# A graph layer's edge loop: fewer loads issued by SyncE, half of the table loads by ScalarE, and the pieces of the MLP values subtracted by TensorE instead of GpSimd

## The chip, the cores and the metric

The kernel runs on one core of a Trainium2 chip. Its time is the device time in microseconds of one execution; a lower one is better. PE is TensorE, DVE VectorE, ACT ScalarE, POOL GpSimd and SP SyncE, which computes nothing and issues DMAs.

## What is computed

412,500 edges join 12,500 nodes with 32 features each. For each edge two small MLPs turn ten edge features into weights, which then mix the features of its two nodes; the results are summed into the receiving node, and the layer ends in a layer norm.

```python
def _mlp(emb, w1, w2):
    h = jax.nn.relu(emb @ w1 / jnp.sqrt(jnp.float32(w1.shape[0])))
    return h @ w2 / jnp.sqrt(jnp.float32(w2.shape[0]))
...
xs, xd = (x[edge_src], x[edge_dst])
w = _mlp(emb, fc1_w1, fc1_w2)          # 512 values per edge, from 16 hidden ones
...
s_t = a1 * (jnp.einsum('eu,euw->ew', s1, Wss) + jnp.einsum('eu,euw->ew', vdot1, Wvv))
v_t = a1 * (jnp.einsum('eu,euw->ew', s1, Wsv)[:, :, None] * sh1[:, None, :] + jnp.einsum('euk,euw->ewk', v1, Wvs))
w2 = _mlp(emb, fc2_w1, fc2_w2)         # 384 values per edge
...
edge_out = jnp.concatenate([jnp.tanh(scal), (vecs * jnp.tanh(gates)[:, :, None]).reshape(E, 24)], axis=1)
edge_out = edge_out * norm[:, None]
return jax.ops.segment_sum(edge_out, edge_dst, num_segments=num_nodes)
```

## The kernel before

**Super tiles and stages.** The edges are sorted by receiver and cut into 403 super tiles of 8 x 128. `periods` runs one body for each: bodies of the first and last tiles written out, and a loop of two bodies (even and odd, for the double buffers) in between. A body works at six stages at once, on six super tiles: `three_on` and `four_on` are three and four ahead (embeddings are loaded and cut), `zero` two ahead (nodes gathered, hidden layer computed), `one` one ahead, `two` in its first products, `three` in its second ones, `four` at its outputs. Each engine has its own program of bodies, in an order written out by hand, and waits on semaphores.

**Pieces.** A float32 value is cut into three bf16 pieces, each the rounded rest of the one before. The pieces of the embeddings are stacked in six groups of ten rows in `emb_stack` (`stack_emb`, line 527, from `emb_parts`), those of the hidden values in six groups of 16 columns in `hid_parts`. ACT rounds (`emb_first`, `emb_second`, `hidden_first`, `hidden_second`), POOL subtracts (`emb_less_first`, `emb_less_second`, `hid_less_first`, `hid_less_second`, lines 829 to 850). ACT's `hidden_out` first brings the hidden values out of the PSUM bank `pa`, which the matmuls of `hidden`, `hidden_near` and `nodes_made` share. SP then turns `hid_parts` with two transposing DMAs, one for each MLP (`turn_hid`, line 546), and PE's `fill` multiplies the result with the second weights.

**Tables.** A receiver's share of the first products comes from a table `t_rows` of one row for each node and hidden value, of which a tile needs a window of eight nodes. `load_near` (line 575) reads the first node of each of the eight tiles from `near_base` into a register and issues a load of that window. PE uses the windows in `receivers`. Every second body also adds 64 nodes to the table (`nodes_made`, `store_nodes`).

**Small loads.** Each body loads the sender indices for the gathers (`load_indices`), the bases (`load_near_bases`), the offsets of the receivers for the one-hot matrices (`load_late`) and the base of the window of sums (`load_late_base`). All of these, the loads of `emb`, the six of the stack and the off rows (`stack_off`) stand in SP's queue; POOL issues the eight gathers of node rows.

**The order around.** PE's body is: fill 1 of `two`, `scalar_sums_turned`, `out_sums` (16 matmuls), `receivers`, `hidden`, `four_sums_turned`, fill 2 of `three`, `vector_sums`, `hidden_near` first half, fill 3, `scalar_sums`, second half, fill 4, `vector_sums_turned`, `scatter`, `nodes_made`, fill 0 of `one`, `gate_sums` (16 matmuls). ACT's is: `scalar_sums_back`, `emb_first`, `out_sums_out` (writes `osum_t`), `node_scalars` (a copy of the receivers' result), `tanh_out`, `hidden_out`, the copies of the node rows, `emb_second`, `hidden_first`, `vector_sums_out`, `near_hidden`, `hidden_second`, `off_hots`, `near_hidden` of the second half, `scalar_sums_out`, `nodes_out`, `one_hot`, `gate_sums_out`.

## Time and profile before

| | |
|---|---|
| median of 3 runs | 9704.65 us (9703.06 to 9709.19) |
| profiled execution | 9652.08 us, its span 9650.3 us |
| PE, PEld, DVE, ACT, POOL busy | 64%, 59%, 49%, 35%, 48% of the span |
| chain of work that ended last | SP's queue 76%, issue 19% |
| granted TensorE clock, mean | 0.788 of full speed |

Issuing DMAs doesn't count as busy, so SP has no share in the table; its queue is seen in the order of time and in the chain. "Issue" is time in which a queue stood at nothing that the profile shows, between two instructions. The lines of the profile are those of the code above.

### The profile page before, as it was taken

The page shows a single profiled execution, that of the slowest core. Times are in us where ns is not written, and L with a number is a line of the kernel's source. Part 1 is how long each engine was busy: PE and PEld are TensorE (multiplying, and loading weights), DVE is VectorE, ACT ScalarE, POOL GpSimd, SP SyncE. Part 2 cuts the span into 40 slices and gives each one's busy share as a digit, 9 for nine tenths or more (in the row PEclk, how much of TensorE's full clock was granted, in tenths as well). Part 3 has the DMA queues.
Part 4 walks back from the last instruction along what each step waited for, and adds up shares of the span by engine and source line. Part 5 has one row for each costly group of instructions (what it writes and reads, how often), then busy time and mean ns, then how long its engine had stood idle before and what let it go on. Part 6 is the DMA issues. An engine that isn't in the chain of part 4 may idle for free.

```text
span 9650.3 us, 223031 instructions
## 1 busy us (share of the span) xinstructions
PE 6180.1 (64%) x59272; PEld 5695.5 (59%) x59272; DVE 4712.0 (49%) x7823; ACT 3364.6 (35%) x10591; POOL 4658.2 (48%) x6483
## 2 busy tenths in 40 slices
PE   2566666666666666666666666666666666666666
PEld 2465665656656566565655656566565665656555
DVE  6344444444444444444444444444444444444445
ACT  2333333333333333333333333333333333333333
POOL 1545454454544545445454454545445454454543
PEclk6777787777878778777787877778777787877877
DMA  4222222222222222222222222222222222222222
GB/s 124 51 54 53 54 55 54 54 53 55 54 54 54 54 55 53 54 54 54 55 53 54 54 54 55 53 54 54 54 55 53 55 53 54 55 54 54 53 54 49
DMA packets 1898444, 535.96 MB, mean 56 GB/s; under 512 B 1783541, under 2 KB 1880551, under 8 KB 1898045
## 3 DMA queue, kind: packets, MB, share of 16 engines
q1 hardware_dynamic: 1795228, 482.38, 22.8%
q0 software_dynamic: 103168, 53.03, 3.8%
q8 instruction: 19, 0.31, 0.0%
q14 instruction: 29, 0.24, 0.0%
HBM read 203.14 MB, written 72.13 MB: 29 GB/s over the span
## 4 chain that ended last, share of the span: by engine, by line
SPq 76%; issue 19%; PE 2%; DVE 1%; DMA 1%; POOL 1%; ACT 0%; POOLq 0%; DVEq 0%; ACTq 0%
SPq L536 19%; SPq L585 15%; SPq L586 14%; SPq L556 10%; SPq L526 4%; SPq L606 2%; SPq L564 2%; SPq L544 2%; SPq L596 2%; SPq L573 2%; SPq L592 1%; SPq L612 1%; PE p L1355 1%; SPq L446 1%; DVE prods L1626 1%
## 5 line engine op out<-in xcount | busy, mean ns | idle before, releaser
L855 POOL DMA_INDIRECT nodes<-x_rows,idx x3224 | 3094.8, 960 | 732.9 <-issue 673.5
L1350 PE MATMUL pw<-w_stack,work 128*128 128x128 bf16 x16120 | 1466.6, 244 | 3032.0 <-DMA work<-hid_parts 2998.4
L1355 PE MATMUL p<-identity,prods 128*128 128x128 f32 x20956 | 3177.5, 314 | 0.6 <-ACT gates_t L1060 0.5
L1350 PEld LDWEIGHTS pw<-w_stack,work 128*128 128x128 bf16 x16120 | 1174.0, 110 | 3390.5 <-issue 3095.3
L1355 PEld LDWEIGHTS p<-identity,prods 128*128 128x128 f32 x20956 | 2886.8, 168 | 1.8 <-issue 1.7
L1689 DVE TENSOR_TENSOR prods<-pw,V 128x1024 f32<-128x1024 f32 x403 | 493.6, 1225 | 2813.4 <-PE pw L1350 2813.4
L832 POOL TENSOR_TENSOR emb_rest<-emb,emb_parts 80x128 f32<-80x128 f32 x403 | 171.6, 426 | 3232.5 <-ACT emb_parts L971 3225.7
L1060 ACT ACTIVATE gates_t<-p 128x128 f32<-128x128 f32 x403 | 111.7, 277 | 4285.8 <-PE p L1355 4285.8
L1775 DVE TENSOR_TENSOR along<-p,r_all 128x192 f32<-128x192 f32 x403 | 144.2, 358 | 1726.2 <-ACT th L1070 1726.2
L1733 DVE TENSOR_TENSOR prods<-pw,M 128x1024 f32<-128x1024 f32 x806 | 976.9, 1212 | 1.6 <-PE pw L1350 1.6
L1337 PE MATMUL pz<-work 128*128 128x64 f32 x6448 | 767.9, 272 | 10.3 <-DMA work<-t_rows 10.0
L1337 PEld LDWEIGHTS pz<-work 128*128 128x128 f32 x6448 | 755.0, 193 | 10.7 <-issue 10.2
L1077 ACT ACTIVATE spare<-node_iota,late_off 128x42 f32<-128x42 f32 x3224 | 747.7, 314 | 0.0
L1741 DVE TENSOR_TENSOR prods<-pw,VT 128x1536 f32<-128x1536 f32 x403 | 705.0, 1749 | 0.5 <-PE pw L1350 0.5
L806 POOL TENSOR_TENSOR msg<-th,w_all 128x128 f32<-128x128 f32 x403 | 164.2, 408 | 755.4 <-ACT th L1070 755.4
L1020 ACT ACTIVATE work<-pa 128x512 f32<-128x512 f32 x806 | 468.2, 581 | 0.8 <-PE pa L1313 0.7
L1706 DVE TENSOR_TENSOR prods<-pw,S 128x512 f32<-128x512 f32 x403 | 278.8, 692 | 269.5 <-PE pw L1350 266.0
L1007 ACT ACTIVATE hid_parts<-hid 128x768 bf16<-128x768 f32 x403 | 336.4, 835 | 0.0
L1434 PE MATMUL p<-spare,msg 128*32 128x42 f32 x6448 | 322.0, 203 | 1.7 <-DVE msg L1785 1.7
L1065 ACT ACTIVATE osum_t<-p 128x256 f32<-128x256 f32 x403 | 154.4, 383 | 474.9 <-PE p L1355 455.0
L1313 PE MATMUL pa<-emb_stack,w_near 96*128 96x512 bf16 x806 | 308.0, 382 | 1.8 <-ACT work L1020 1.3
L1038 ACT ACTIVATE prods<-pz 128x64 f32<-128x64 f32 x403 | 114.4, 284 | 557.9 <-PE pz L1337 557.9
(174 smaller groups left out, 8232.2 us busy)
## 6 DMA issues: line engine op xcount, KB each, us to landing
work<-t_rows SPq DMA_DIRECT2D x3224, 32.0 KB
t_rows<-t_stage SPq DMA_DIRECT2D x205, 256.0 KB
nodes<-x_rows,idx POOLq DMA_INDIRECT x3224
emb_stack<-emb_parts SPq DMA_DIRECT2D x2418, 20.0 KB
emb<-in_emb_t SPq DMA_DIRECT2D x403, 40.0 KB
work<-hid_parts SPq DMA_TRANSPOSE x806, 2.9
idx<-rec SPq DMA_DIRECT2D x403, 4.0 KB, 1.7
near_base<-base_rows SPq DMA_DIRECT2D x403, 0.0 KB
```

Of the source, the lines that this page charges most:

```text
L536: sp.dma_start(emb_stack[K1 * g:K1 * g + K1, p, :].rearrange("k (c e) -> k c e", c=G), emb_parts[:, p, part, :]).then_inc(stack_in[p], 16)
L556: sp.dma_start_transpose(hid_t[:, layer, p, :, :], hid_parts[:, p, layer * G:layer * G + G, :].rearrange("e t k -> e (t k)")).then_inc(tur ...
L585: first = nc.sync.value_load(near_base[0:1, p, t:t + 1], min_val=0, max_val=N - 1)
L586: sp.dma_start(t_near[:, p, t, :], t_rows[bass.ds(first * H, NEAR * H), :]).then_inc(t_near_in[p], 16)
L855: nc.gpsimd.indirect_dma_start(nodes[:, p, t, :], None, x_rows, bass.IndirectOffsetOnAxis(ap=idx[:, p, t:t + 1], axis=0)).then_inc(nodes_i ...
L1077: nc.scalar.activation(off_hot[:, t, :], node_iota[:, :], ACT.Square, bias=off[:, t:t + 1]).then_inc(off_hot_done, 1)
L1337: mm = nc.tensor.matmul(z[:, :, t, :], hid_near[:, P * t:P * t + P], t_near[:, a.par, t, :].rearrange("p (c w) -> p c w", w=C), start=(t = ...
L1350: mm = nc.tensor.matmul(pw[:, slot, t, :], hid_t[:, layer, a.par, t, :], w2_stack[:, lo:lo + W], start=True, stop=True)
L1355: return nc.tensor.matmul(out, column, identity[:, :], start=first, stop=last, is_transpose=True)
L1689: nc.vector.tensor_tensor(prod_v01.rearrange("p u k t w -> p k t u w"), weights(0, ring, 0).unsqueeze(1).broadcast_to([P, 2, G, C, C]), V[ ...
L1733: nc.vector.tensor_tensor(prod_g[:, :, half, :, :].rearrange("p u t w -> p t u w"), weights(2 + half, ring), M[:, a.par, :, :].unsqueeze(3 ...
L1741: nc.vector.tensor_tensor(prod_o[:, :, 0:3, :, :].rearrange("p u k t w -> p k t u w"), weights(4, ring, 1).unsqueeze(1).broadcast_to([P, 3 ...
```

## The change

- **Stacks.** `store_emb` stores the three pieces of `emb_parts` with one DMA in a DRAM tensor `emb3`. In the next body `stack_emb` waits for it and loads the stack with three DMAs, of three, two and one pieces. The off rows are loaded one body later too.
- **Small loads.** One record of indices and offsets for four super tiles (`load_records`) and one row of bases for four (`load_bases`) replace four loads; each body loads them anew, and the users take the slot of their stage. `load_bases` waits for the readers of the buffer on ACT and DVE (`windows_begun`, `window_begun`).
- **Table loads.** `load_windows` reads four bases with one load of registers and issues four windows. SP does this for tiles 0 to 3, and ACT, in a `load_near` of its own behind `out_sums_out`, for tiles 4 to 7.
- **Pieces of the hidden values.** They stay in PSUM. ACT writes the first piece three times straight from there, with ReLU and a factor a little under one, so that the rest stays positive; PE adds the piece times minus identity to the bank (`hidden_less`); ACT writes the second piece twice, PE subtracts it, ACT writes the third. `hidden_out` and POOL's two subtractions are gone, and `hidden_near` waits for the third piece (`hid_c`) where it waited for `hid_done`. The factor for the ten inputs moves into the second weights.

SP, in the loop's first body, from the table loads to the stacks. Before, with the first of the eight table loads and the end of the last:

```order
L585 TENSOR_LOAD near_base [waits t_stored]
L585 ISA x2
L586 ISA
L586 DMA work<-t_rows 128x64
...
L586 DMA work<-t_rows 128x64
L573 ISA
L573 DMA near_base<-base_rows 1x8
L556 DMA_TRANSPOSE work<-hid_parts 128x8x128 [waits hid_c,hid_a,hid_b,filled_b]
L606 ISA [waits off_hot_done]
L606 DMA late_off<-rec 128x8
L536 DMA emb_stack<-emb_parts 10x8x128 [waits hid_mm,emb_c,near_mm]
L536 DMA emb_stack<-emb_parts 10x8x128 x5
```

After, from the same place, with the first of four table loads, up to the stacks in the next body:

```order
L522 TENSOR_LOAD near_base [waits t_stored]
L522 ISA x8
L525 ISA
L525 DMA work<-t_rows 128x64
...
L612 ISA [waits windows_begun]
L612 DMA near_base<-base_rows 1x32
L581 DMA_TRANSPOSE work<-hid_parts 128x8x128 [waits hid_c,hid_a,hid_b,filled_b]
L450 ISA [waits emb_c]
L547 DMA emb3<-emb_parts 80x3x128 [waits stack_in1]
L581 DMA_TRANSPOSE work<-hid_parts 128x8x128 [waits hid_c,hid_a,hid_b,filled_e]
L560 DMA emb_stack<-emb3 30x1024 [waits near_mm]
L560 DMA emb_stack<-emb3 20x1024
```

Four issues and seven register loads are gone, late offsets too; one store stands where six stack issues stood, and the three that fill the stack stand in the next body.

ACT, between the copy of the out sums (`osum_t`) and the first piece of the hidden values. Before:

```order
L1065 ACTIVATE osum_t<-p2 128x256 [waits four_back,osum_sum]
L1036 REGISTER_ALU
L1038 ACTIVATE prods<-pz 128x64 [waits sv_done,d_mm]
L1070 ACTIVATE th<-p1 128x128 [waits msg_done,four_back]
L991 REGISTER_ALU
L996 ACTIVATE hid<-pa 128x8x2x16 [waits hid_a,hid_rest_done,hid_mm]
```

After, where three more pairs like the last `ISA` and `DMA` stand ahead of the copy from `pz`:

```order
L1088 ACTIVATE osum_t<-p2 128x256 [waits four_back,osum_sum]
L450 REGISTER_ALU [waits near_base_in1,d_mm]
L522 TENSOR_LOAD near_base [waits t_stored]
L522 ISA x8
L525 ISA
L525 DMA work<-t_rows 128x64
L1061 ACTIVATE prods<-pz 128x64 [waits sv_done,d_mm]
L1093 ACTIVATE th<-p1 128x128 [waits msg_done,four_back]
L1029 ACTIVATE hid_parts<-pa 128x16x48 [waits turned_in10,turned_in00,hid_mm]
```

The table loads came in ahead of the dot copy and tanh, and the first piece (line 1029) follows tanh at once, out of `pa`.

PE, from the turning of the four sums to fill 3. Before:

```order
L1427 MATMUL p1<-identity,gates_t 128x128 [waits msg_done]
L1429 MATMUL p1<-identity,osum_t 128x128 x2
L1350 MATMUL pw<-w2_stack,work 128x128 [waits turned_in11,pss_done]
L1350 MATMUL pw<-w2_stack,work 128x128 x7
L1355 MATMUL p2<-identity,prods 128x128 [waits pv_done]
L1355 MATMUL p2<-identity,prods 128x128 x3
L1313 MATMUL pa<-emb_stack,w1_near 128x512 [waits t_out,hid_done]
L1350 MATMUL pw<-w2_stack,work 128x128 [waits turned_in11,pc_done,pvv_done]
```

After:

```order
L1472 MATMUL p1<-identity,gates_t 128x128 [waits msg_done]
L1474 MATMUL p1<-identity,osum_t 128x128 x2
L1346 MATMUL pa<-hid_parts,minus_bf 128x256 [waits hid_a]
L1395 MATMUL pw<-w2_stack,work 128x128 [waits turned_in11,pss_done]
L1395 MATMUL pw<-w2_stack,work 128x128 x7
L1400 MATMUL p2<-identity,prods 128x128 [waits pv_done]
L1400 MATMUL p2<-identity,prods 128x128 x3
L1346 MATMUL pa<-hid_parts,minus_bf 128x256 [waits hid_b]
L1358 MATMUL pa<-emb_stack,w1_near 128x512 [waits t_out,hid_c,off_in1]
L1395 MATMUL pw<-w2_stack,work 128x128 [waits turned_in11,pc_done,pvv_done]
```

A subtraction stands ahead of fill 2 and another behind the vector sums, each with a wait for ACT.

```diff
-    c1 = 1.0 / (4.0 * 32.0 ** 0.5)
-    c2 = 1.0 / (4.0 * 4.0)
+    c1 = float(K1) ** -0.5 / (4.0 * 32.0 ** 0.5)
+    c2 = float(K1) ** -0.5 / (4.0 * 4.0)
+    below = 1.0 - 2.0 ** -8
...
+    emb3 = nc.dram_tensor("emb3", [2, 3, K1, SUPER], BF16, kind="Internal").ap()
...
-        hid_rest = sb("hid_rest", [P, 2 * G, H])
+        minus_bf = sb("minus_bf", [P, P], BF16)
...
+        def load_windows(eng, p, t0):
+
+            half = G // 2
+            _, firsts = nc.values_load_multi_w_load_instructions(
+                near_base[0:1, p, 3 * G + t0:3 * G + t0 + half], engines=[eng.engine], min_val=0, max_val=N - 1)
+            for t in range(half):
+                eng.dma_start(t_near[:, p, t0 + t, :], t_rows[bass.ds(firsts[t] * H, NEAR * H), :]
+                              ).then_inc(t_near_in[p], 16)
...
-            def stack_emb(a, is_general=True):
+            def store_emb(a):
 
                 p = a.par
-                if not is_general:
+                sp.wait_ge(emb_c, a.n(1, 1))
+                sp.sem_inc(begun, 1)
+                wait(sp, stack_in[p], a.before(2).k(16 * 3))
+                sp.dma_start(emb3[p].rearrange("a k (c e) -> (k c) a e", c=G), emb_parts[:, p, :, :]).then_inc(emb_stored[p], 16)
+
+            def stack_emb(a, is_general):
+
+                p = a.par
+                sp.wait_ge(emb_stored[p], a.k(16))
+                sp.sem_inc(begun, 1)
+                if is_general:
+                    wait(sp, hid_mm, a.before(2).n(1, 1))
+                else:
                     wait(sp, near_mm, a.before(2).n(2, 2))
-                sp.wait_ge(emb_c, a.n(1, 1))
-                wait(sp, hid_mm, a.before(2).n(1, 1))
-                for g, part in enumerate((0, 1, 2, 0, 1, 0)):
-                    sp.dma_start(emb_stack[K1 * g:K1 * g + K1, p, :].rearrange("k (c e) -> k c e", c=G),
-                                 emb_parts[:, p, part, :]).then_inc(stack_in[p], 16)
+                first = 0
+                for parts in (3, 2, 1):
+                    sp.dma_start(emb_stack[K1 * first:K1 * (first + parts), p, :],
+                                 emb3[p, 0:parts].rearrange("a k e -> (a k) e")).then_inc(stack_in[p], 16)
+                    first += parts
...
+            def load_records(at, i, is_general):
+
...
+                if i is None or 0 <= i + 1 < NS:
+                    sp.wait_ge(nodes_in[1 - p], At(at.b, at.d + 1).k(16 * G))
+                    sp.sem_inc(begun, 1)
+                if not is_general:
+                    wait(sp, off_hot_done, at.before(2).n(G, G))
+                    sp.sem_inc(begun, 1)
+                sp.dma_start(near[:, p, lo:hi, :], rec[:, bass.ds(at.index() + lo, hi - lo), :]).then_inc(near_in[p], 16)
+
...
+            def load_bases(at, i):
+
...
+                wait(sp, window_begun, at.n(1, -2))
+                sp.sem_inc(begun, 1)
+                wait(sp, windows_begun, at.n(1, 1) if i is None else min(i + 1, NS))
+                sp.sem_inc(begun, 1)
+                sp.dma_start(near_base[:, p, G * lo:G * hi],
+                             base_rows[:, bass.ds((at.index() + (lo - 1)) * G, (hi - lo) * G)]).then_inc(near_base_in[p], 16)
...
-                for t in range(G):
-                    first = nc.sync.value_load(near_base[0:1, p, t:t + 1], min_val=0, max_val=N - 1)
-                    sp.dma_start(t_near[:, p, t, :], t_rows[bass.ds(first * H, NEAR * H), :]).then_inc(t_near_in[p], 16)
+                load_windows(nc.sync, p, 0)
...
                     if four_on is not None:
                         load_emb(four_on)
-                    if three_on is not None:
-                        load_indices(three_on, is_general)
-                    if three is not None and not is_general:
-                        load_late_base(three)
+                    load_records(at, i, is_general)
+                    if three_on is not None and is_general:
+                        load_destinations(three_on)
                     if one is not None and not is_general:
                         load_near(one)
-                    if three_on is not None and not is_general:
-                        load_near_bases(three_on)
+                    if not is_general:
+                        load_bases(at, i)
                     if one is not None and i != -1:
                         turn_hid(one, 0)
-                    if two is not None:
-                        load_late(two, is_general)
+                    if two is not None and is_general:
+                        load_late_destinations(two)
                     if three_on is not None:
-                        stack_emb(three_on, is_general)
-                        if not is_general:
-                            stack_off(three_on)
+                        store_emb(three_on)
...
-            def hid_less_first(a):
...
-            def hid_less_second(a):
-                pool.wait_ge(hid_b, a.n(1, 1))
-                nc.gpsimd.tensor_tensor(hid_parts[:, a.par, :, KH - H:KH], hid_rest[:, :, :],
-                                        hid_parts[:, a.par, :, 3 * H:4 * H], ALU.subtract).then_inc(hid_c, 1)
...
-            def hidden_out(a, is_general):
+            def parts_of(a):
+                return hid_parts[:, a.par, :, 0:KH].rearrange("p a (g h) -> p a g h", h=H)
+
+            def hid_of(copies):
+                return hid_ps.unsqueeze(2).broadcast_to([P, 2 * G, copies, H])
+
+            def hidden_first(a, is_general):
+
                 act.wait_ge(hid_mm, a.n(1, 1))
-                wait(act, hid_rest_done, a.before(2).n(1, 1))
-                wait(act, hid_a, a.before(2).n(1, 1))
-                if is_general:
-                    wait(act, t_prods_done, a.before(2).n(G, G))
-                nc.scalar.activation(hid[:, a.par, :, :].rearrange("p (l t) h -> p t l h", l=2),
-                                     hid_ps.rearrange("p t (l h) -> p t l h", l=2), ACT.Relu,
-                                     scale=float(K1) ** -0.5).then_inc(hid_done, 1)
-
-            def hidden_first(a):
-                act.wait_ge(hid_done, a.n(1, 1))
                 for layer in range(2):
                     wait(act, turned_in[layer][a.par], a.before(2).k(16))
                 if a.static and a.b * 2 + a.d == 0:
                     act.wait_ge(parts_zero, 3)
-                parts = hid_parts[:, a.par, :, 0:KH].rearrange("p a (g h) -> p a g h", h=H)
-                nc.scalar.activation(parts[:, :, 0:3, :], hid[:, a.par, :, :].unsqueeze(2).broadcast_to([P, 2 * G, 3, H]),
-                                     ACT.Copy).then_inc(hid_a, 1)
+                if is_general:
+                    wait(act, t_prods_done, a.before(2).n(G, G))
+                    nc.scalar.activation(hid[:, a.par, :, :], hid_ps, ACT.Relu).then_inc(hid_done, 1)
+                nc.scalar.activation(parts_of(a)[:, :, 0:3, :], hid_of(3), ACT.Relu, scale=below).then_inc(hid_a, 1)
 
             def hidden_second(a):
-                parts = hid_parts[:, a.par, :, 0:KH].rearrange("p a (g h) -> p a g h", h=H)
-                act.wait_ge(hid_rest_done, a.n(1, 1))
-                nc.scalar.activation(parts[:, :, 3:5, :], hid_rest[:, :, :].unsqueeze(2).broadcast_to([P, 2 * G, 2, H]),
-                                     ACT.Copy).then_inc(hid_b, 1)
+                act.wait_ge(hid_less, a.n(2, 1))
+                nc.scalar.activation(parts_of(a)[:, :, 3:5, :], hid_of(2), ACT.Relu, scale=below).then_inc(hid_b, 1)
+
+            def hidden_third(a):
+                act.wait_ge(hid_less, a.n(2, 2))
+                nc.scalar.activation(parts_of(a)[:, :, 5, :], hid_ps, ACT.Relu).then_inc(hid_c, 1)
...
+            def load_near(a):
+
+                p = a.par
+                act.wait_ge(near_base_in[p], a.k(16))
+                act.sem_inc(begun, 1)
+                wait(act, d_mm, a.before(2).n(1, 1))
+                act.sem_inc(begun, 1)
+                wait(act, t_stored, a.before(1).k(16, 16 * (LEAD - 1)))
+                act.sem_inc(begun, 1)
+                load_windows(nc.scalar, p, G // 2)
+                act.sem_inc(windows_begun, 1)
...
+                    if one is not None and fast:
+                        load_near(one)
                     if two is not None:
                         node_scalars(two)
                     if four is not None:
                         tanh_out(four)
                     if zero is not None:
-                        hidden_out(zero, is_general)
+                        hidden_first(zero, is_general)
                     if one is not None:
                         row_scalars(one)
                         row_vectors(one)
                     if three_on is not None:
                         emb_second(three_on)
                     if zero is not None:
-                        hidden_first(zero)
+                        hidden_second(zero)
                     if two is not None:
                         vector_sums_out(two)
+                    if zero is not None:
+                        hidden_third(zero)
                     if one is not None and fast:
                         near_hidden(one, 0)
-                    if zero is not None:
-                        hidden_second(zero)
                     if marking is not None:
...
+            def hidden_less(a, piece, made):
+
+                pe.wait_ge(made, a.n(1, 1))
+                slot = (0, 3)[piece]
+                nc.tensor.matmul(hid_ps, minus_bf[:, :], hid_parts[:, a.par, :, slot * H:slot * H + H], start=False,
+                                 stop=True, skip_group_check=True).then_inc(hid_less, 1)
...
                         hidden(zero, is_general)
                     if four is not None:
                         four_sums_turned(four, windows, more)
+                    if zero is not None:
+                        hidden_less(zero, 0, hid_a)
                     if three is not None:
                         if two is not None:
                             pe.wait_ge(pss_done, two.n(1, 1))
...
                         fill(three, 2, at.par)
                     if two is not None:
                         vector_sums(two, four)
+                    if zero is not None:
+                        hidden_less(zero, 1, hid_b)
                     if one is not None and fast:
                         hidden_near(one, 0)
...
-                        dve.wait_ge(late_base_in[four.par], four.k(16))
+                        dve.wait_ge(near_base_in[1 - four.par], four.k(16, 32 if four.par else 16))
                         dve.sem_inc(begun, 1)
-                        first = nc.vector.value_load(late_base[0:1, four.par, 0:1], min_val=0, max_val=N - 1)
+                        first = nc.vector.value_load(near_base[0:1, 1 - four.par, 0:1], min_val=0, max_val=N - 1)
+                        dve.sem_inc(window_begun, 1)
```

## Rows read from the trace of the kernel before

**Rows 1.** The page: busy time of the engines (parts 1, 3 and 4)

```profile
PE 6180.1 (64%) x59272; PEld 5695.5 (59%) x59272; DVE 4712.0 (49%) x7823; ACT 3364.6 (35%) x10591; POOL 4658.2 (48%) x6483
...
q1 hardware_dynamic: 1795228, 482.38, 22.8%
...
SPq 76%; issue 19%; PE 2%; DVE 1%; DMA 1%; POOL 1%; ACT 0%; POOLq 0%; DVEq 0%; ACTq 0%
```

**Rows 2.** Who waited for whom: engine, line, releaser, us, times, longest

```profile
PE pw L1350 <- DMA work<-hid_parts: 2998.4, 401, 9.5
```

**Rows 3.** SP in order of time: start us, us, line, operation

```profile
5007.03 0.59 SPq L592 DMA_DIRECT2D t_rows<-t_stage  x1
5009.27 0.90 SPq L526 DMA_DIRECT2D emb<-in_emb_t  x1
5010.48 0.36 SPq L564 DMA_DIRECT2D idx<-rec  x1
...
5012.87 8.29 SPq L586 DMA_DIRECT2D work<-t_rows  x8
...
5024.18 4.94 SPq L536 DMA_DIRECT2D emb_stack<-emb_parts  x6
...
5055.61 0.90 SPq L526 DMA_DIRECT2D emb<-in_emb_t  x1
```

**Rows 4.** Lines 585 and 586, table loads: duration ns min/median/max

```profile
L585 SPq TENSOR_LOAD <-near_base x16: 263/268/465, 5011.9 to 5041.9; - x16
...
L586 SPq DMA_DIRECT2D work<-t_rows x2904: 337/338/368, 1002.6 to 9399.3; - x194
```

**Rows 5.** PE in order of time: two bodies at full clock, one at half

```profile
3360.16 0.61 PE L1350 MATMUL pw<-w_stack,work 128*128 128x128 bf16 x8
3360.61 0.39 PE L1396 MATMUL pz<-halves,st_t 128*128 128x64 f32 x2
3360.83 1.92 PE L1355 MATMUL p<-identity,prods 128*128 128x128 f32 x16
...
3364.71 0.33 PE L1427 MATMUL p<-identity,gates_t 128*128 128x128 f32 x1
...
3365.09 0.61 PE L1350 MATMUL pw<-w_stack,work 128*128 128x128 bf16 x8
...
3366.85 0.38 PE L1313 MATMUL pa<-emb_stack,w_near 96*128 96x512 bf16 x1
...
3371.12 0.38 PE L1254 MATMUL pa<-wt,xt 48*64 48x256 bf16 x2 [0.48 <-ACT work L1020]
...
3379.63 3.62 PE L1355 MATMUL p<-identity,prods 128*128 128x128 f32 x16
```

**Rows 6.** ACT in order of time, the same body

```profile
3362.79 0.38 ACT L1065 ACTIVATE osum_t<-p 128x256 f32<-128x256 f32 x1 [1.20 <-PE p L1355]
...
3365.29 0.28 ACT L1070 ACTIVATE th<-p 128x128 f32<-128x128 f32 x1 [0.49 <-PE p L1429]
...
3366.42 0.84 ACT L1007 ACTIVATE hid_parts<-hid 128x768 bf16<-128x768 f32 x1
...
3367.42 0.60 ACT L1020 ACTIVATE work<-pa 128x512 f32<-128x512 f32 x1
...
3368.64 1.86 ACT L1077 ACTIVATE spare<-node_iota,late_off 128x42 f32<-128x42 f32 x8
```

**Rows 7.** GpSimd by line, 500 to 9500 us: busy us, mean ns, idle before

```profile
L844 POOL TENSOR_TENSOR hid_rest<-hid,hid_parts 128x256 f32<-128x256 f32 x388 | 264.5, 682 | 8.1
```

**Rows 8.** The page, DMA issues: KB each, median us to landing

```profile
work<-hid_parts SPq DMA_TRANSPOSE x806, 2.9
idx<-rec SPq DMA_DIRECT2D x403, 4.0 KB, 1.7
```

**Rows 9.** PE in order of time, before the loop

```profile
204.31 0.60 PE L1254 MATMUL p<-wt,xt 48*64 48x256 bf16 x2 [4.43 <-ACT t_stage L1025]
...
217.57 0.38 PE L1254 MATMUL p<-wt,xt 48*64 48x256 bf16 x2 [3.09 <-ACT t_stage L1025]
```

119 lines of the change are left out of this document (57 added, 62 removed).

## The prediction

> **What bounds the kernel now.** I read the engine shares first, then the chain of work that ended last, then who waited for whom, and last the order in time of two bodies of the loop. No compute engine is busy for more than 64% of the span, and the chain stands on SP's queue for 76% of it [rows 1]. PE's largest wait, 2998 us, is for the transposing DMA that SP issues [rows 2]. The order in time shows why: SP goes from issue to issue without a pause, and two bodies take 5055.61 - 5009.27 = 46.34 us [rows 3]. That is 23.17 us for each of the 403 super tiles, so 9,338 us of the span; the rest, about 310 us, is the part before and after, which the change hardly touches. SP's queue is therefore a serial program of issue times. An issue taken off it is worth its full time until another loop is longer.
>
> **What leaves SP.** One body of SP as it is [rows 3]: six stack issues in 4.94 us (0.82 each), eight table issues in 8.29 us (1.14 from one to the next), of which the register load is 0.27 [rows 4].
> - Four table loads go to ACT: 4 x 1.14 = 4.6. The four that stay share one register load, so three are saved: 3 x 0.27 = 0.8.
> - Six stack issues become three: -2.5. In their place one store to DRAM. No row shows it. The nearest are the 64-partition store at 0.59 (5007.03) and the 80-partition load at 0.90 (5009.27); with its wait I take 1.1, and 0.6 to 2 as ends.
> - The small loads of the late base and of the late offsets go. Each is like the index load, 0.36 long (5010.48); with what surrounds them I take 0.7 and 0.6.
> - More waits on semaphores: +0.3.
> SP's own work becomes 23.2 - 4.6 - 0.8 - 2.5 + 1.1 - 0.7 - 0.6 + 0.3 = 15.4 us a body. If nothing else set the pace, that would be 403 x 7.8 = 3,140 us less.
>
> **The next loop: PE, ACT and DVE.** I take a body where PE ran at the full clock and set 0 at its turning of the four sums, 3364.71 [rows 5]. From that point to the matmul of nodes_made (3371.12) are 6.4 us, to the fill behind it some 6.7. From such a fill to the next zero: the fill itself 0.45 (as from 3360.16 to 3360.61), sixteen gate sums 1.8 (as the out sums, 1.92 long and overlapping), and 3364.71 - 3360.16 = 4.55 for fill, out sums, receivers and hidden. That is 6.8, so a round without stall would be 13.5 us. Today the gate sums after the stall run at half clock (3.62 in place of 1.92), which then ends.
>
> *ACT's four table loads.* They stand behind osum_t, which ends at 3363.17, that is -1.5 [rows 6], and in front of the dot copy, tanh and the first pieces. On SP such a block costs one load, four pairs of register checks and four issues: 4 x 1.14 - 3 x 0.27 = 3.8 us. No row shows ACT issuing a DMA, and its queue also has activations to pass on, so I take a little over SP: 4.1. Ends: 1.3, where it would fit in the time for which ACT waits for the receivers' matmuls anyway, and 6.0, if each issue cost a stack issue's 0.82. With 4.1 ACT is free at 2.6, tanh begins at 2.85 rather than 0.6 (3365.29), and the first pieces, 0.84 long, are out at 3.9 [rows 6].
>
> *PE's two subtractions.* Each is one matmul of 256 columns, about 0.2 us, half of the 0.38 of the 512-column one [rows 5]. The price is the waits in PE's order. The first stands before the fill of kind 2, which today starts 0.38 after the zero; now it waits for ACT's first pieces (3.9) and the fill starts at 4.2: +3.8, of which some 2.5 are ACT's loads. The second stands behind the vector sums, at 6.0, and ACT's second pieces are out at about 5.0. But hidden_near must now wait until ACT has read the bank a third time, since the values stay in PSUM: 6.2 + 0.4 = 6.6, so it starts at 6.7 where it started at 2.1. Behind it ACT copies it (0.6), makes the off hots (1.86), copies the second half (0.6) [rows 6]: with PE's 0.38 and the hand-overs 3.6 us to nodes_made, at 10.3, and the next fill at 10.5. The round is 10.5 + 6.8 = **17.3 us**. DVE (4712 / 403 = 11.7 us busy a body) is carried along, and ACT comes to 8.3 + 4.1 = 12.4 [rows 1].
>
> *GpSimd.* Two operations of 0.68 us leave each body [rows 7]. I cost their removal at nothing: POOL is busy 11.6 us a body today [rows 1], and with the pauses between its gathers its round is some 13 us. If ACT's work were free, POOL would still not be first.
>
> *Does SP come back?* SP waits every second body for ACT's node copy (0.85 after that fill), then issues store and xt (2.2), three stacks (2.7), off rows (0.6), emb (1.2), records (0.7), the first table load with its waits (1.35), the rest (2.9), bases (0.85, as the index load with its waits): 12.5; the transpose lands 2.9 later [rows 8]. That is 0.85 + 12.5 + 2.9 = 16.3, against 17.3 for which PE does not need it. So it is hidden, with 1.0 us to spare in two bodies.
>
> **The sum.** 403 x (23.17 - 17.3) = 2,370 us. The profiled execution took 9652.08, so its like would be 7,282. The median of the runs is 52.6 above that execution; 9704.65 - 2370 = **7,335 us**.
>
> **A rule weighed.** The packets of SP's queue take 22.8% of the 16 DMA engines' time [rows 1]. The Trainium skill, DMA: Bandwidth & Descriptors, section "Issuing engines are not separate DMA queues", says that a second issuing engine saves only the time to initiate a DMA, usually small beside the DMA itself. It would let one expect almost nothing from the move. Here the first half agrees with the trace and the second does not: the issue time is the bound.
>
> **Rivals.**
> 1. *ACT's loads are cheap, or much of them is hidden.* With 1.3 us for the block the PE round is 14.5, and SP's loop decides: (14.5 + 16.3) / 2 = 15.4 a body, 403 x 7.8, so 6,570 us. Between that and 17.3 lies 6,900 for a block of 3.0. For it: ACT waits there today. Against it: SP's issue rows are steady at 0.338.
> 2. *Issues collide.* Four issues on ACT fall into the stretch where SP issues its own; each waiting for one of 0.34 to 0.8 us adds about 1.9: 19.2 a body, 9704.65 - 403 x 3.97 = 8,105. The rows can't show it, as only SP issues such DMAs. The Trainium skill, Perfetto Trace Analysis, section "DMA Instruction - HWDGE (DVE, Sync)", says that the descriptor generator is shared and locked for one sequencer at a time; no trace here shows a lock wait.
> 3. *The clock falls in the new gap.* PE would idle from 0.55 to 4.0, some 3.4 us a body. After an idle stretch of 3.09 us the trace has a pair of matmuls in 0.38 us, at full clock; after 4.43 us it has 0.60 for the same pair [rows 9]. If the clock falls to its lower level in each body, fill and sums after the gap lose what they lose today, 1.7 + 0.4: 19.4 a body, 8,185 us.
> 4. *SP is in the way again.* If store, stack loads and landings cost 4 us a pair more than I took, the two bodies take 17.3 + 20.3: 18.8 each, 7,945 us.
> 5. *Slower than before.* The embedding pieces now go to DRAM and back. SP waits in its queue for the store to land before it issues the stacks, and everything behind stands. A body is then 13 us plus the landing time. It passes 23.17 when landing takes over 10.2 us; at 12 it gives 25.0 a body, 10,440 us. The nearest landing is 1.7 us for a small load [rows 8], so this is far away.
> 6. *No change.* If SP's issues were long because the transfers behind them were full, fewer issues would not help: 9,705 us. Constant issue times and idle DMA engines speak against it.
>
> **Chances.** The forecast, with block costs from 3.2 to 5.0 us (16.4 to 18.2 a body, 6,980 to 7,700 us), 0.50. Rival 1 0.17, rival 2 0.10, rival 3 0.11, rival 4 0.07, rival 5 0.03, rival 6 0.02. The range must take in rivals 2 and 3 and most of the way to rival 1, since no row shows an ACT issue: 6,750 to 8,190 us. Left out are about half of rival 1, rivals 5 and 6 and the far end of 3 and 4, less than 0.2. Within 0.2% is what a measurement of this kernel can tell from no change; faster than that 0.95, within it 0.02, slower 0.03.
>
> **What the profile after would show.** SP has pauses, with waits for ACT's node copy, and no longer holds the chain; PE's wait for the transposes (2998 us) falls to a few hundred or less. In its place stand a PE wait of about 3.4 us a body ahead of the first subtraction, on ACT's first pieces, and a short one ahead of hidden_near. ACT's dot copy starts about 4 us after osum_t rather than 1.7. The gate sums take 1.9 us. POOL waits longer, not shorter. The mean granted clock is above 0.9. I would be wrong if ACT's four issues take under 2 us (then 6,600 to 6,900), if the matmuls behind the gap take twice as long, or if PE still waits for the transposes.

## The result, and the profile after

The changed kernel takes **9094.31 us** (median of 4 runs, 9075.28 to 9110.34) against 9706.92 us: ratio 0.9368, 95% interval 0.9347 to 0.9389. It is faster, but by 6% and not by the 24% that I forecast (7335 us), and outside my range (6,750 to 8,190). Its profiled execution took 9084.12 us. With the 313 us around the loop (9650.3 - 403 x 23.17) a body takes (9081.9 - 313) / 403 = 21.8 us; I had taken 17.3.

The page of the changed kernel: engine shares, granted clock in 40 slices, DMA queues (q10 is the new one, which ScalarE issues to) and the chain that ended last. The rows of before are [rows 1]:

```profile
PE 6666.9 (73%) x60078; PEld 6007.7 (66%) x60078; DVE 4733.8 (52%) x7823; ACT 3365.5 (37%) x10591; POOL 4138.0 (46%) x5678
...
PEclk8788878788888888888888878887888888888877
...
q1 hardware_dynamic: 1428533, 464.10, 22.6%
...
q10 hardware_dynamic: 232128, 52.93, 2.6%
...
PE 56%; issue 18%; ACTq 13%; ACT 8%; another core or an unknown queue 3%; DVE 1%; SPq 1%; POOL 0%; DMA 0%; DVEq 0%; POOLq 0%
```

SP's queue has left the chain (76% before, 1% now), and PE holds it with ACT. The bound has moved as forecast. The waits say where it is dear (engine, line, releaser: us in all, times, longest):

```profile
DVE prods L1782 <- remote: 1923.5, 299, 7.2
...
PE pa L1346 <- ACT hid_parts L1029: 998.6, 400, 3.8
PE pa L1358 <- issue: 948.1, 403, 5.1
ACT vs_t L1066 <- remote: 889.3, 211, 6.4
...
SPq L580 <- PE pw L1395: 1937.7, 322, 8.5
```

No row is left of PE's wait for the transposes [rows 2]. PE waits 2.5 us a body for ACT's first pieces (L1346), as foreseen. The rest I had not foreseen: 2.4 us ahead of `hidden_near` (L1358), and DVE and ACT waiting for "remote", which means that nothing in the records had just ended when they were let go.

One body in order of time shows such a release: PE, then ACT, then POOL.

```profile
5002.37 0.33 PE L1472 MATMUL p<-identity,gates_t 128*128 128x128 f32 x1
...
5005.34 0.28 PE L1346 MATMUL pa<-hid_parts,minus_bf 128*128 128x256 bf16 x1 [2.42 <-ACT hid_parts L1029]
...
5005.90 1.48 PE L1400 MATMUL p<-identity,prods 128*128 128x128 f32 x12
5007.22 0.27 PE L1346 MATMUL pa<-hid_parts,minus_bf 128*128 128x256 bf16 x1
5010.44 0.58 PE L1358 MATMUL pa<-emb_stack,w_near 96*128 96x512 bf16 x1 [2.95 <-issue]
...
5016.31 0.38 PE L1291 MATMUL pa<-wt,xt 48*64 48x256 bf16 x2 [0.73 <-ACT work L1043]
...
5009.69 0.38 ACT L1066 ACTIVATE vs_t<-p 128x256 f32<-128x256 f32 x1 [3.25 <-remote]
...
5005.40 0.98 POOL L880 DMA_INDIRECT nodes<-x_rows,near  x1 [0.23 <-issue]
5006.69 0.94 POOL L880 DMA_INDIRECT nodes<-x_rows,near  x1 [0.30 <-issue]
...
5008.25 0.96 POOL L880 DMA_INDIRECT nodes<-x_rows,near  x1 [0.16 <-issue]
```

The vector sums (L1400) and the subtraction behind them (L1346) are over at 5007.5 by PE's own rows, yet ACT, which waits for nothing else, copies the sums at 5009.69. The trace's semaphore events have the sums' signal at 5009.66, 2.28 us behind the recorded end, and the subtraction's at 5009.70, 0.03 behind it, though that matmul is 0.27 long. So the signals are held and then come in a bunch. ACT starts 0.02 us behind the signal, so it is really let go that late. I call a TensorE completion **late** when its signal comes over 0.7 us behind the recorded end. Between 500 and 8500 us the changed kernel has 2067 late ones; the kernel before has 7.

The count takes the first recorded event of the semaphore at or behind the end, within 12 us, and some events have no record: 7 of 100 in the changed kernel, 1.5 in the kernel before, up to 24 elsewhere, none in the kernels without gathers. Where two matmuls raise one semaphore, the first is then counted late by the record of the second. In 306 of 368 bodies of the changed kernel this is so for the first half of `hidden_near`, though ACT's copy, which waits for it, starts 0.04 us behind its end. If each record is given only to the last matmul that it can belong to, 1746 late ones are left in the changed kernel and none of the 7 in the kernel before. In e2, e4 and e5c below 1266, 1083 and 528 are left, elsewhere nearly all; no reading below hangs on the difference.

The Trainium skill, Perfetto Trace Analysis, section "Summary: the profiler window per engine type", says that a TensorE end in the profile is estimated. Here the kernel before agrees with the estimate to 0.01 us throughout, so an end that differs by 2 us is a finding.

### The profile page after: what moved, and what is told of

It reads as the page before. It is cut to its first block, busy times and chain, and to the rows that moved or that the text cites. A ratio compares the mean times of both kernels' runs of the same rounds, so it can differ in the third digit from the quotient of the medians.

```text
span 9081.9 us, 221656 instructions
## 1 busy us (share of the span) xinstructions
PE 6666.9 (73%) x60078; PEld 6007.7 (66%) x60078; DVE 4733.8 (52%) x7823; ACT 3365.5 (37%) x10591; POOL 4138.0 (46%) x5678
## 4 chain that ended last, share of the span: by engine, by line
PE 56%; issue 18%; ACTq 13%; ACT 8%; another core or an unknown queue 3%; DVE 1%; SPq 1%; POOL 0%; DMA 0%; DVEq 0%; POOLq 0%
PE p L1400 31%; PE pw L1395 12%; ACTq L525 7%; ACTq L522 4%; PE pa L1358 4%; ACT hid_parts L1029 3%; PE pa L1346 2%; PE p L1479 2%; ACT spare L1100 2%; PE pa L1291 2%; ACT work L1043 1%; PE pz L1441 1%; DVE prods L1675 1%; PE pz L1423 1%
## 5 line engine op out<-in xcount | busy, mean ns | idle before, releaser
L880 POOL DMA_INDIRECT nodes<-x_rows,near x3224 | 3087.9, 958 | 851.9 <-issue 804.5
L1400 PE MATMUL p<-identity,prods 128*128 128x128 f32 x20956 | 3216.2, 316 | 0.6 <-ACT gates_t L1083 0.5
L1400 PEld LDWEIGHTS p<-identity,prods 128*128 128x128 f32 x20956 | 2879.0, 167 | 1.2 <-DVE prods L1796 0.7
L1395 PE MATMUL pw<-w_stack,work 128*128 128x128 bf16 x16120 | 1557.8, 253 | 7.2 <-DVE prods L1762 3.1
L1395 PEld LDWEIGHTS pw<-w_stack,work 128*128 128x128 bf16 x16120 | 1280.5, 115 | 288.8 <-issue 157.7
L1358 PE MATMUL pa<-emb_stack,w_near 96*128 96x512 bf16 x806 | 411.2, 510 | 948.1 <-issue 948.1
L1346 PE MATMUL pa<-hid_parts,minus_bf 128*128 128x256 bf16 x806 | 286.4, 355 | 1013.9 <-ACT hid_parts L1029 998.6
L1346 PEld LDWEIGHTS pa<-hid_parts,minus_bf 128*128 128x128 bf16 x806 | 92.1, 114 | 1109.0 <-ACT hid_parts L1029 1092.6
L1358 PEld LDWEIGHTS pa<-emb_stack,w_near 96*128 96x128 bf16 x806 | 92.7, 115 | 1094.9 <-issue 1094.9
L1100 ACT ACTIVATE spare<-node_iota,near 128x42 f32<-128x42 f32 x3224 | 748.7, 318 | 0.0
L1066 ACT ACTIVATE vs_t<-p 128x256 f32<-128x256 f32 x403 | 154.8, 384 | 1538.3 <-remote 889.3
```

What stands on the lines that cost most here:

```text
L880: nc.gpsimd.indirect_dma_start(nodes[:, p, t, :], None, x_rows, bass.IndirectOffsetOnAxis(ap=near[:, 1 - p, 3, t:t + 1], axis=0)).then_inc ...
L1100: nc.scalar.activation(off_hot[:, t, :], node_iota[:, :], ACT.Square, bias=off[:, t:t + 1]).then_inc(off_hot_done, 1)
L1346: nc.tensor.matmul(hid_ps, minus_bf[:, :], hid_parts[:, a.par, :, slot * H:slot * H + H], start=False, stop=True, skip_group_check=True).t ...
L1358: nc.tensor.matmul(near_ps, w1_near[:, :, :].rearrange("k n h -> k (n h)"), emb_stack[:, p, 512 * half:512 * half + 512], start=True, stop ...
L1395: mm = nc.tensor.matmul(pw[:, slot, t, :], hid_t[:, layer, a.par, t, :], w2_stack[:, lo:lo + W], start=True, stop=True)
L1400: return nc.tensor.matmul(out, column, identity[:, :], start=first, stop=last, is_transpose=True)
```

## The experiments

All against the kernel before on the same chip. "Body" is (span - 313) / 403, "late" as above, "clock" the mean granted TensorE clock. e6c ran on a chip on which the kernel before takes 9651.8 us; where the others ran it would take 7652 x 9707 / 9652 = 7696 us, which I use in differences. e6c, e11 and e14 leave the gathers out, so their node rows are not those of the senders and their results are other values.

| kernel | us | ratio (95%) | body | late | clock |
|---|---|---|---|---|---|
| before | 9707 | 1 | 23.2 | 7 | 0.79 |
| the change | 9094 | 0.937 (0.935 to 0.939) | 21.8 | 2067 | 0.81 |
| e1 POOL subtracts | 7737 | 0.795 (0.791 to 0.799) | 18.5 | 1444 | 0.91 |
| e2 all table loads on SP | 9202 | 0.948 (0.947 to 0.950) | 22.0 | 1543 | 0.84 |
| e3 both, SP's part alone | 7815 | 0.805 (0.803 to 0.806) | 18.7 | 1238 | 0.87 |
| e4 before, PE subtracts | 10956 | 1.129 (1.127 to 1.131) | 26.4 | 1327 | 0.77 |
| e6c the change, no gathers | 7652 | 0.793 (0.792 to 0.794) | 18.2 | 0 | 0.86 |
| e5c the change, gathers apart | 7869 | 0.811 (0.809 to 0.812) | 18.7 | 609 | 0.88 |
| e7c e1, gathers apart (0.2 us) | 7444 | 0.765 (0.761 to 0.769) | 17.8 | 1620 | 0.93 |
| e9 e1, gathers apart (0.4 us) | 7346 | 0.756 (0.755 to 0.758) | 17.6 | 1385 | 0.92 |
| e10 e4, gathers apart | 9714 | 1.0005 (0.9996 to 1.0015) | 23.3 | 21 | 0.83 |
| e8 e1, real work between gathers | 7095 | 0.730 (0.728 to 0.732) | 16.8 | 1692 | 0.95 |
| e12 e8, all table loads on SP | 7512 | 0.775 (0.773 to 0.776) | 17.9 | 838 | 0.90 |
| e11 e8, no gathers | 6487 | 0.668 (0.667 to 0.670) | 15.3 | 0 | 0.98 |
| e13 e8 and gathers apart | 6813 | 0.703 (0.700 to 0.705) | 16.0 | 489 | 0.96 |
| e14 e6c, ACT's loads later | 7963 | 0.821 (0.819 to 0.823) | 19.0 | 0 | 0.87 |

### Which part loses the time (e1 to e4)

e1 puts the two subtractions back on POOL, with `hidden_out`; e2 moves all eight table loads to SP; e3 does both; e4 is the kernel before with TensorE's subtraction.

```diff
 # e1 (POOL's body; ACT and PE as before the change)
                         gathers(zero, (2,))
+                        hid_less_first(zero)
                         gathers(zero, (3,))
...
                         gathers(zero, (4,))
+                        hid_less_second(zero)
                         gathers(zero, (5,))
 # e2
                 load_windows(nc.sync, p, 0)
+                load_windows(nc.sync, p, G // 2)
...
-                    if one is not None and fast:
-                        load_near(one)
```

> The changed kernel with one part undone: GpSimd subtracts the pieces of the MLP values again (ScalarE copies them from SBUF as before), SyncE and ScalarE load as in the change. In the changed kernel a body takes 21.8 us instead of the 17.3 us I had taken, and TensorE's vector sums are reported 1.7 us (mean) after the end that the matmul records show, the fills of layer 1 about 2 us; in the kernel before that lateness was 0.01 us. Theory A: the subtraction on TensorE is the cause (TensorE waits there for ScalarE twice, its clock falls, and its work ends late). Then without it the lateness is gone, the clock is above 0.9, and the body is bound by SyncE's queue (15.4 us) or a little over: 6600 to 7600 us. Rival B: the fewer and larger transfers, or ScalarE's loads, disturb TensorE. Then lateness stays at 1.5 us or more and the time at 8800 us or more.

> The changed kernel with one part undone: all eight table loads are issued by SyncE, none by ScalarE. ScalarE's block of 3.4 us is gone, SyncE's queue grows by about 2 to 3 us to some 18 us a body, which is under the 21.8 us that a body takes. Theory A (the subtraction on TensorE makes the loss): TensorE's lateness stays, since the waits for ScalarE stay; a body is shorter by at most the 3.4 us of the block: 7700 to 8900 us. Rival B (ScalarE's DMA issues disturb TensorE and the others): lateness falls below 0.3 us and the time to 7300 us.

> Only SyncE's part of the change: fewer and larger loads, all eight table loads still on SyncE, subtraction on GpSimd. Both theories that blame TensorE's subtraction or ScalarE's loads expect no lateness here and a body bound by SyncE's queue of some 18 us: 7300 to 7900 us. If the larger transfers or the way over DRAM disturb TensorE, the lateness is here too and the time is above 8500 us.

> The kernel before with one part of the change alone: TensorE instead of GpSimd subtracts the pieces, all loads as before. SyncE's queue of 23.2 us a body still sets the pace. Theory A: TensorE's completions come late here too (over 1 us at the vector sums), and since a body with them takes up to 21.8 us the time stays about 9700, up to 2 per cent more. Rival B: no lateness (below 0.1 us), time 9700.

The subtraction costs 9094 - 7737 = 1357 us with ACT's loads and 9202 - 7815 = 1387 us without them, 3.4 us a body each time, and 1250 us in the kernel before. ACT's loads are worth 78 to 108 us there. But theory A, as I put it, fell: e1 came out above its range, and in e1 and e3 completions are late too, though PE subtracts nothing in them. And e4 was 13% slower where I expected 0 to 2. SP waits for nobody in e4's loop; its own issuing had become slower. SP in order of time, e4:

```profile
5011.53 11.22 SPq L587 DMA_DIRECT2D work<-t_rows  x8
```

The same eight issues take 8.29 us in the kernel before [rows 3]; over all bodies the medians are 10.8 and 8.2. Something that comes with TensorE's new order held up TensorE's signals and SyncE's issues alike.

What the late completions have in common is POOL. In these five kernels (the change, e1 to e4) a completion whose recorded end lies beside the second or third of gathers that directly follow each other (1.25 us from start to start) is late in 74 to 100 of 100 cases; where no gather had begun in the last 3 us, in none. (The expectations below say 83 to 100; e3's share is 74.) The kernel before has such pairs too, 691 of them, but not one with a matmul beside it. POOL, then PE, kernel before:

```profile
5016.26 0.96 POOL L855 DMA_INDIRECT nodes<-x_rows,idx  x1 [0.16 <-issue]
5017.53 0.94 POOL L855 DMA_INDIRECT nodes<-x_rows,idx  x1 [0.30 <-issue]
...
5015.77 0.38 PE L1254 MATMUL pa<-wt,xt 48*64 48x256 bf16 x2 [0.39 <-ACT work L1020]
5024.98 1.01 PE L1350 MATMUL pw<-w_stack,work 128*128 128x128 bf16 x8 [8.84 <-DMA work<-hid_parts]
```

The pair ran while PE stood waiting for the transposes. That wait, 7.4 us a body, was what kept the two apart.

The same pair says one thing more. It runs beside SP's eight table loads (5012.87 to 5021.16), and these take their usual 8.29 us [rows 3]. Between 500 and 8500 us SP has 2,558 register instructions beside the second gather of such a pair in the kernel before, and none of its 18,298 takes over 0.18 us; in e4 1,256 take over 0.3 us, the longest 0.92. So two gathers that touch hold up nobody by themselves here. It takes PE's work beside them, as in e1 and e3, which have the same two pairs a body as the kernel before.

### Is it the gathers (e6c, e5c, e10, e7c, e9)

e6c leaves the gathers out. e5c keeps them and puts a dummy addition between those that touch; e10 does the same to e4; e7c and e9 do it to e1, at its two pairs.

```diff
 # e6c
-                    nc.gpsimd.indirect_dma_start(
-                        nodes[:, p, t, :], None, x_rows,
...
+                sp.dma_start(nodes[:, a.par, :, :], x_rows[0:P * G, :].rearrange("(p g) f -> p g f", g=G)).then_inc(nodes_in[a.par], 16)
 # e5c, e10 (pad: one tensor_tensor of 128x256)
                         gathers(zero, (2,))
+                        if not is_general:
+                            pad(zero, 0)
                         gathers(zero, (3,))
```

> The changed kernel without GpSimd's eight gathers: SyncE loads 1024 rows in their stored order with one plain load instead, so the node rows that are used are not those of the edges' senders. Everything else is as in the change. In the traces so far a TensorE completion is late only while gathers follow each other directly (83 to 100 of 100 beside the second or third of a run, none where no gather began in the last 3 us). Theory A (such gathers hold up TensorE's completions and SyncE's issue): no late completions at all; the body is what my prediction had, 17.3 us or less: 6800 to 7600 us. Rival B (the two only coincide; the loss is in TensorE's order and waits): TensorE's completions stay late (over 1000 of them), the time stays above 8500 us.

> The changed kernel with one addition: GpSimd does a dummy addition (128x256, written to a tile that nobody reads, some 0.7 us) between gathers that otherwise follow each other directly (ahead of gathers 3, 5 and 6 and behind 7). In the traces so far a TensorE completion is late in 83 to 100 of 100 cases where a second or third gather runs directly behind another, never where no gather began in the last 3 us. Theory A (gathers that follow each other directly hold up TensorE's completions and SyncE's issue): late completions fall from 2067 to under 700, and the time from 9094 to 7600 to 8600 us. Rival B (only that gathers run at all matters, however they are spaced, or they only coincide): lateness stays, and 2.7 us a body of GpSimd's work more makes it the same or slower: 9050 to 9400 us.

> The kernel in which GpSimd subtracts and the rest is as in the change (7737 us), with a short dummy addition (128x64, some 0.2 us) between the two pairs of gathers that still follow each other directly (ahead of gather 6 and behind 7). Theory A: the late completions (1444) fall to less than half, SyncE waits less, 7000 to 7600 us. Rival B: no change or slower, 7700 to 7850 us.

> The kernel before with the subtraction on TensorE alone (10956 us, where SyncE never waits and its own issuing took 26.3 us a body in place of 23.2), with the dummy additions of 128x256 between the gathers. Theory A: SyncE's issue is no longer held up, and the time is back near the kernel before, 9700 to 9950 us. Rival B (TensorE's subtraction costs this by its own waits): 10800 us or more.

> The kernel with GpSimd's subtraction and dummy additions at the two pairs, the additions now 128x128 (some 0.4 us) instead of 128x64 (0.2 us; 7444 us, 1620 late completions). Theory A: the share of late completions falls with the distance of the gathers: under 1200 late, 7250 to 7450 us. Rival C (distance beyond 1.4 us makes no difference): 1500 or more late, 7440 to 7550 us.

Without gathers no completion is late, and 9094 us become 7696 (above the 7600 that I expected at most). With all eight gathers in place and *more* work on POOL, 9094 become 7869 us. e10 is the plainest: 10956 us become 9714, the time of the kernel before to 0.05%, and SyncE's issues are back, though some 1,600 of TensorE's completions lie beside a gather there (21 of all are late). POOL and SP in order of time, e4 (two gathers that touch, behind them a third) and then e10:

```profile
5015.45 0.95 POOL L845 DMA_INDIRECT nodes<-x_rows,idx  x1 [0.16 <-issue]
5016.71 0.94 POOL L845 DMA_INDIRECT nodes<-x_rows,idx  x1 [0.30 <-issue]
5017.96 0.94 POOL L845 DMA_INDIRECT nodes<-x_rows,idx  x1 [0.30 <-issue]
```

```profile
5000.89 8.29 SPq L588 DMA_DIRECT2D work<-t_rows  x8
...
5001.63 0.95 POOL L852 DMA_INDIRECT nodes<-x_rows,idx  x1 [0.16 <-issue]
5002.60 0.62 POOL L846 TENSOR_TENSOR hid<-identity 128x256 f32<-128x256 f32 x1
5003.38 0.95 POOL L852 DMA_INDIRECT nodes<-x_rows,idx  x1 [0.16 <-issue]
```

So rival B is out: the gathers that follow each other, beside PE's work, are a cause and not a companion. e7c and e9 gained 293 and 390 us, less than a full cure. e7c's late ones did not fall to half as expected (1444 to 1620); each was shorter, 2.7 us in the mean for e1 and 1.8 for e7c.

### Real work in place of dummy work (e8, e11, e12, e13, e14)

POOL has eight arithmetic operations a body for eight gathers. e8 takes e1 and only puts them in another order, one between any two gathers.

```diff
 # e8
+                    if two is not None:
+                        along_rest(two)
                         gathers(zero, (0,))
                         emb_less_first(three_on)
-                        along_rest(two)
                         gathers(zero, (1,))
                         along_last(two)
+                        gathers(zero, (2,))
                         messages_scalar(four, windows, more)
-                        gathers(zero, (2,))
-                        hid_less_first(zero)
                         gathers(zero, (3,))
-                        emb_less_second(three_on)
+                        hid_less_first(zero)
                         gathers(zero, (4,))
-                        hid_less_second(zero)
+                        emb_less_second(three_on)
                         gathers(zero, (5,))
+                        hid_less_second(zero)
                         gathers(zero, (6,))
```

> No dummy work: the kernel in which GpSimd subtracts (7737 us), with GpSimd's real additions put in another order so that one of them stands between any two gathers (the first of the sums along the edge ahead of gather 0, the last ahead of 2, the scalar messages ahead of 3, the first subtraction ahead of 4, the second part of the embedding ahead of 5, the second subtraction ahead of 6). Theory A (gathers that follow each other directly hold up TensorE's completions and SyncE's issue): the pair of 1.25 us spacing is gone, late completions fall below those of the kernel with dummy additions (1620), 7200 to 7500 us. Rival C (what remains of the lateness comes from gathers at any spacing, and the later subtraction costs a chain more): 7500 to 7800 us.

> The kernel in which GpSimd subtracts and its real additions stand between the gathers (7095 us, 1692 late completions, SyncE's short records still there), without the gathers: SyncE loads 1024 rows in their stored order with one plain load, so the node rows used are not those of the senders. It shows what a body costs with nothing of the effect left. Theory A (what is left of the lateness in the 7095 us comes from the gathers): no late completion, SyncE's queue bounds, 15.4 us and its one load more, 15.8 us a body: 6500 to 6850 us. Rival C (a chain over ScalarE and TensorE bounds by now): 6900 to 7100 us.

> The kernel of 7095 us with all eight table loads on SyncE, none on ScalarE. It shows what ScalarE's share of the loads is worth once the rest no longer covers it. ScalarE's block is 3.4 us a body, SyncE's queue gets four loads more, some 2.2 us a body. If SyncE's queue is the bound: 7500 to 8000 us. If ScalarE's block costs more than it gives: 6800 to 7050 us.

e8 takes **7095 us**, 27% less than before and 22% less than the change, a little under what theory A said. It still has 1692 late completions. e11, the same without gathers, has none and takes 6487 us, so the gathers still cost about 608 us (1.5 us a body). Part of this is their own time on POOL and no hold-up: SP waits 810 us for the embedding pieces that POOL makes behind gathers in e8, and 191 in e11. At 15.3 us a body e11 comes out where my prediction put SP's loop, 15.4, but its chain is shared by several engines, so it isn't shown that SP alone bounds it:

```profile
SPq 27%; issue 19%; PE 18%; ACT 13%; ACTq 9%; DMA 9%; POOL 2%; DVE 2%; DVEq 0%; POOLq 0%
```

e12 says what ACT's share of the loads is worth when nothing else covers it: 7512 - 7095 = 417 us, 1.0 us a body. With all on SP, SP hardly waits and holds 50% of the chain. The Trainium skill, DMA: Bandwidth & Descriptors, section "Issuing engines are not separate DMA queues", says that a second issuing engine saves only the time to initiate the DMAs, usually small beside the DMA itself. Here the move is worth 6%, and 1% where late completions bound (e2 against the change).

e13 spaces e8's gathers further with six dummy additions of 128x64. e14 takes e6c and moves ACT's table loads from ahead of the dot copy to behind the first pieces.

```diff
 # e13
                         gathers(zero, (1,))
...
+                            pad(zero, 2)
                         gathers(zero, (2,))
 # e14
-                    if one is not None and fast:
-                        load_near(one)
                     if two is not None:
                         node_scalars(two)
...
                         hidden_first(zero, is_general)
+                    if one is not None and fast:
+                        load_near(one)
```

> The kernel of 7095 us (GpSimd subtracts, its real additions between the gathers) with short dummy additions (128x64, 0.2 us) beside the shorter of them, so that gathers start some 1.8 us apart or more. Over the traces so far a completion beside a gather that begins under 1.3 us behind the one before is late in 92 of 100, at 1.65 to 1.75 us in 83, at 1.75 to 1.85 us in 14, from 2.1 us in none. Theory A (distance decides): under 600 late completions and 6600 to 6950 us; without gathers it was 6487. Rival C (GpSimd's queue, by then some 14 us a body, becomes what is late next): 7050 to 7300 us.

> The kernel with TensorE's subtraction and without gathers (7652 us; node rows are not those of the senders), with ScalarE's four table loads behind the first pieces in place of ahead of the dot copy. TensorE waits 2.5 us a body for the first pieces and 2.5 us ahead of the vector sums' copy back there. If the block of 3.4 us ahead of the pieces is what makes the subtraction dear, as my prediction took it: 2 to 3 us a body less, 6500 to 6900 us. If it is the chain of four hand-overs between TensorE and ScalarE, in which the block now stands ahead of the second pieces: 7400 to 7700 us.

e13 is the fastest of the kernels with gathers: **6813 us**, ratio 0.703, with 489 late completions. Over the twelve kernels with gathers traced up to e12, among completions that lie beside a gather, the late share by that gather's distance from the one before is:

```
start to start, us   <1.3   1.3-1.5  1.5-1.65  1.65-1.75  1.75-1.85  1.85-2.1  2.1-3   >3
completions          3207   2133     8154      2698       7272       219       563     6367
late, of 100         92     61       38        83         14         9         0       3
```

It falls with distance, though not evenly (the 83 are often the third of a closer group), so distance alone is not the whole rule. The kernel before and e10 have next to none late at 1.5 to 1.85 us, where e5c has 20 to 38 of 100 from 1.65 us up. With each record counted once the row reads 91, 62, 37, 83, 13, 9, 0, 0.

e14 went the other way: 7963 - 7696 = 267 us slower than e6c, beyond both expectations. PE's wait for the first pieces falls from 1002 to 431 us, but in its place PE waits 801 us for the second pieces and DVE longer for the fill. The block of loads is paid wherever it stands inside the chain of hand-overs.

## Why the prediction was wrong, point by point

**SP's part: right in kind, a little dear, and near e11 by luck.** I had 15.4 us of SP's own work a body. e11's body is 15.3, but SP waits in 1.3 of these and issues one load more than the change, so its own work there is 14.0 with that load. In the changed kernel SP waits 2572 us, 6.4 a body, and 21.8 - 6.4 = 15.4 is again my figure, but how much of that is hold-up these runs don't tell. The terms that were too dear: three stack issues take 1.10 us (I had 2.7), one store 0.34 (I had 1.1 with its wait). SP's waits in e11:

```profile
SPq L643 <- ACT t_stage L1064: 198.2, 201, 1.1
SPq L545 <- POOL emb_parts L880: 191.2, 201, 7.9
SPq L580 <- PE pw L1404: 130.8, 204, 9.5
```

SP in order of time, the changed kernel, against [rows 3]:

```profile
5001.88 1.93 SPq L525 DMA_DIRECT2D work<-t_rows  x4
...
5008.28 0.34 SPq L547 DMA_DIRECT2D emb<-emb_parts  x1
...
5019.88 1.10 SPq L560 DMA_DIRECT2D emb_stack<-emb  x3
```

Rivals 4, 5 and 6 are out with it. SP does pause, but mostly for PE's fill (L580, 1937.7 us), and only 87 us for ACT's node copy, the wait that I had named.

**ACT's block: a little dear.** I took 4.1 us; ACT stands still 3.4. ACT in order of time:

```profile
5000.45 0.38 ACT L1088 ACTIVATE osum_t<-p 128x256 f32<-128x256 f32 x1 [1.22 <-PE p L1400]
5002.08 1.87 ACTq L525 DMA_DIRECT2D work<-t_rows  x4
5004.19 0.28 ACT L1061 ACTIVATE prods<-pz 128x64 f32<-128x64 f32 x1 [3.35 <-issue]
```

Four issues in 1.87 us are as quick as SP's own four (1.93), and the two run at the same time, from 5002.08 and from 5001.88, so rival 2 (issues collide) has nothing for it here. "Under 2 us" for the four issues was one of my signs of being wrong, with 6,600 to 6,900 us behind it; it came true, but the register load and its checks in front of them (the rest of the 3.4) made the block nearly what I had taken.

**PE's order: right, where the gathers are away.** A body of e6c, from the turning of the four sums to the next:

```profile
5004.83 0.32 PE L1474 MATMUL p<-identity,gates_t 128*128 128x128 f32 x1
...
5007.89 0.28 PE L1348 MATMUL pa<-hid_parts,minus_bf 128*128 128x256 bf16 x1 [2.52 <-ACT hid_parts L1031]
...
5008.77 2.77 PE L1402 MATMUL p<-identity,prods 128*128 128x128 f32 x12
...
5012.33 0.38 PE L1360 MATMUL pa<-emb_stack,w_near 96*128 96x512 bf16 x1 [0.58 <-issue]
...
5015.87 0.40 PE L1293 MATMUL pa<-wt,xt 48*64 48x256 bf16 x2
5016.20 0.62 PE L1397 MATMUL pw<-w_stack,work 128*128 128x128 bf16 x8
...
5022.96 0.33 PE L1474 MATMUL p<-identity,gates_t 128*128 128x128 f32 x1
```

PE has the first pieces 3.1 us behind the turning (I had 3.9). The fill behind `nodes_made` comes at 11.4 (I had 10.5), and from there to the next turning are 6.8 (I had 6.8): 18.1 in all against 17.3. What is longer is the clock: the vector sums take 2.77 us at the lower level where they take 1.48 in the row of the changed kernel at full clock.

**The clock (rival 3): right in kind.** I argued from [rows 9] that a gap of 3 us leaves the clock up, since the two matmuls behind it ran at full speed. So do the first here, at 5007.89; the half clock comes behind them, from 5008.25 for 3.41 us in the clock's records. The row that I read was too short to see it: in the kernel before too, the half clock begins at 219.29, 1.3 us behind the end of the pair at 217.57. In the body of the changed kernel it begins at 5010.24, just ahead of `hidden_near`. Two hand-overs a body then leave the clock at 0.86 (e6c) against 0.98 without TensorE's subtraction (e11). The subtraction costs 7696 - 6487 = 1209 us, 3.0 us a body, of which I had forecast 1.9 (17.3 - 15.4).

**GpSimd: the step that failed.** I wrote "I cost their removal at nothing", because POOL is not first. The sum had no term for what POOL's gathers do to the work beside them. POOL is not first now either. But its two subtractions stood between gathers, and without them four of the eight gathers of a body follow another one directly (1,472 between 500 and 8500 us; two a body before, 691). And I had not asked what the wait for the transposes, which the change was to remove, had kept apart. Of the 1759 us by which the forecast missed, 9094 - 7696 = 1398 are gone when the gathers are; this is an upper bound for the hold-up, since e6c also leaves out the gathers' own work. Spacing the gathers, with all of them in place, gives back 1225 (e5c). The other 361 us are PE's round and its clock, as above. How much of the loss is due to the two operations taken away, and how much to PE's work having moved beside the gathers, stays open. With both subtractions still on POOL the gathers cost nearly as much, 7737 - 6487 = 1250 us (e1 to e11, which also has POOL's operations in e8's order), so the missing spacers alone do not explain it. In the body shown at the start it is the stretch from 5007.5 to 5010.44: `hidden_near` comes 8.1 us behind the turning although the vector sums ran at full clock (7.5 in e6c, where they ran at half), and behind it the half clock and a second hold-up (the `dots` end at 5013.90, their signal comes at 5015.51) bring `nodes_made` to 13.9 in place of 11.0.

**Signs.** As said before the run: no wait for the transposes, PE's wait ahead of the first subtraction (2.5 us, I had 3.4), gate sums 1.9 us. Not so: the clock (0.81, I had over 0.9), the short wait ahead of `hidden_near` (2.4 us), and POOL waiting longer (12.3 us idle a body, 12.4 before).

## What to carry to other kernels

An operation that "costs nothing" on an engine with time to spare can still be the spacer between two others; before removing it, look at what then stands side by side, on that engine and beside the others' busy stretches. The same holds for a long wait that a change removes. Where many gathers are issued by GpSimd, put its other work between them: the order alone was worth 642 us here (e1 to e8), and moving work off GpSimd onto TensorE cost 1357 us (e1 to the change). When a trace shows signals that come late, look at what the waiting engine did as well, since a missing record looks like a late one.
